# A transformer layer on one core: from all experts for every token to two experts per token, in seats of 128 rows

## What is computed

```python
x = x + _layernorm(attention(_layernorm(x), wq, wk, wv, wo, biases))
x = x + _layernorm(ffn(_layernorm(x)))

def ffn(x):                                # H = 256, I = 176, E = 8, K = 2
    probs = softmax(einsum('bsh,he->bse', x, Wr))
    topk_w, topk_idx = top_k(probs, K)
    topk_w = topk_w / sum(topk_w)
    combine = einsum('bsk,bske->bse', topk_w, one_hot(topk_idx, E))
    g = einsum('bsh,ehi->besi', x, Wg)     # the reference: all experts, all tokens
    u = einsum('bsh,ehi->besi', x, Wu)
    y = einsum('besi,eih->besh', silu(g) * u, Wd)
    return einsum('bse,besh->bsh', combine, y)
```

## Time and profile before

| | |
|---|---|
| median of three runs | 2106.59 us |
| the profiled execution | 2106.23 us, its span 2104.5 us |
| TensorE busy | 2035.6 us, 97% of the span |
| VectorE, GpSimd, ScalarE busy | 84%, 73%, 67% |
| mean granted clock of TensorE | 0.986 |
| last `add_out` of attention | starts 1854.25 us after the span's start |
| first of the 44 expert steps | starts at 1885.56 us |

### The profile page before, as it was taken

The page is one execution under the profiler, slowest core; times in us unless marked ns, Lnnn a source line. Parts: engine busy times, 40 slices in busy tenths (PEclk is TensorE's granted clock), DMA queues, the critical chain, the costliest instruction groups (busy, mean ns, idle before and its releaser), DMA issues.

```text
span 2104.5 us, 32745 instructions
## 1 busy us (share of the span) xinstructions
PE 2035.6 (97%) x11188; PEld 1755.3 (83%) x11188; DVE 1775.5 (84%) x2651; ACT 1404.8 (67%) x2575; POOL 1546.5 (73%) x1329
## 2 busy tenths in 40 slices
PE   7999999999999999999999999999999999849998
PEld 5888888888888888888888888888888888738887
DVE  6889889988989888988999898989898889865553
ACT  5777767776777667776776677776777677624443
POOL 2679778886879777877787787877797678846333
PEclk9999999999999999999999999999999999969999
DMA  4667657766667666765777666766676567730000
GB/s 101 159 154 177 160 141 164 171 164 161 147 155 177 154 146 159 180 159 140 165 169 160 148 160 151 176 154 148 153 181 157 136 151 171 165 112 1 11 11 21
DMA packets 216584, 298.24 MB, mean 142 GB/s; under 512 B 44897, under 2 KB 85345, under 8 KB 216417
## 3 DMA queue, kind: packets, MB, share of 16 engines
q1 hardware_dynamic: 216416, 296.15, 59.9%
HBM read 25.46 MB, written 2.10 MB: 13 GB/s over the span
## 4 chain that ended last, share of the span: by engine, by line
PE 74%; SPq 8%; DVE 7%; POOL 5%; ACT 3%; DMA 2%; issue 1%; POOLq 0%; DVEq 0%; ACTq 0%
PE ps_a L617 16%; PE ps_s L498 13%; PE ps_s L500 13%; PE ps_s L499 13%; PE ps_a L618 8%; SPq L317 7%; POOL pT_both L410 4%; PE ps_a L498 2%; PE ps_a L500 2%; PE ps_a L499 2%; DVE probs L1086 2%; ACT probs L821 2%; DVE part_max L1067 1%; PE ps_a L751 1%; PE ps_a L754 1%
## 5 line engine op out<-in xcount | busy, mean ns | idle before, releaser
L410 POOL TENSOR_TENSOR pT_both<-pT,pT_both 128x512 fp32r<-128x512 f32 x1024 | 1301.1, 1301 | 350.4 <-ACT pT_both L834 348.2
L617 PE MATMUL ps_a<-pT_both,v_hi 128*128 128x512 f32 x2048 | 741.5, 395 | 3.8 <-POOL pT_both L410 3.6
L834 ACT ACTIVATE pT_both<-pT 128x512 fp32r<-128x512 f32 x1024 | 610.7, 630 | 195.5 <-DMA pT<-probs 163.2
L821 ACT ACTIVATE probs<-ps_s,shift 128x1024 f32<-128x1024 f32 x512 | 566.3, 1109 | 259.0 <-DVE shift L1076 258.5
L1086 DVE STREAM_TRANSPOSE probs<-probs 128x1024 f32<-128x1024 f32 x512 | 619.1, 1229 | 55.0 <-ACT probs L821 54.2
L1067 DVE TENSOR_REDUCE part_max<-ps_s 128x1 f32<-128x1024 f32 x512 | 612.4, 1215 | 16.1 <-PE ps_s L500 9.5
L618 PE MATMUL ps_a<-pT_both,v_lo 128*128 128x256 f32 x2048 | 574.5, 281 | 0.0
L617 PEld LDWEIGHTS ps_a<-pT_both,v_hi 128*128 128x128 f32 x2048 | 385.3, 188 | 86.8 <-POOL pT_both L410 3.7
L498 PE MATMUL ps_s<-kT_hi,qT_hi 128*128 128x512 f32 x1024 | 405.0, 396 | 11.6 <-ACT probs L821 8.2
L500 PE MATMUL ps_s<-kT_hi,qT_lo 128*128 128x512 f32 x1024 | 403.6, 394 | 0.0
L499 PE MATMUL ps_s<-kT_lo,qT_hi 128*128 128x512 f32 x1024 | 403.0, 394 | 0.0
(11 more groups left out here) (159 smaller groups left out, 2859.5 us busy)
## 6 DMA issues: line engine op xcount, KB each, us to landing
pT<-probs SPq DMA_DIRECT2D x2048, 128.0 KB, 2.5
pT<-in_L_attn_x SPq DMA_DIRECT2D x4, 512.0 KB, 5.7
codes<-in_L_attn_wk_codes SPq DMA_DIRECT2D x16, 128.0 KB, 2.4
scales<-in_L_attn_wk_scales SPq DMA_DIRECT2D x64, 32.0 KB, 3.0
codes<-in_L_attn_wo_codes SPq DMA_DIRECT2D x16, 128.0 KB, 2.3
scales<-in_L_attn_wo_scales SPq DMA_DIRECT2D x64, 32.0 KB, 1.9
x<-in_L_attn_x SPq DMA_DIRECT2D x4, 512.0 KB, 7.1
layer_out<-x SPq DMA_DIRECT2D x8, 256.0 KB, 2.1
```

The lines of the kernel that those rows point to most:

```text
L410: pool.tensor_tensor(pT_lo[:, p, :].rearrange("p (i n) -> p i n", i=Q4), pT[:, s % 2, g, :, t:t + 2, :].rearrange("p i t q -> p i (t q)"), ...
L617: nc.tensor.matmul(out_both, v_hi[:, k, h % 2, :], both[:, :, :, t, :], start=k == 0, stop=False)
L821: nc.scalar.activation(out, src, ACT.Exp, bias=shift[:, s % SLOTS, r:r + 1], scale=SCALE, accum_out=sums[:, s % SLOTS, r, g:g + 1])\
L834: nc.scalar.activation(pT_hi[:, p, :].rearrange("p (i n) -> p i n", i=Q4), pT[:, s % 2, g, :, t:t + 2, :].rearrange("p i t q -> p i (t q)" ...
```

## The change

The tokens are put into two parts of eight tiles of 128 rows. For each part the router works out, for each token, its two experts and a row for each in a table in device memory. The table of a part has 23 seats of 128 rows (2·8 + 8 − 1: enough however the tokens fall), each of which belongs to one expert; both parts have 46. GpSimd sends each token's normed row to its two rows with indirect DMAs (`send`: two for each tile, 32 in all). Then a loop over the 46 seats loads a seat, turns it (`turn_x`), reads the seat's expert into a register (`expert_of`), multiplies with that expert's weights at an address from the register (`gate_up`: six matmuls of 352 columns), turns the hidden rows (`turn_h`), multiplies down (`down`: six of 256 columns) and stores the seat. GpSimd fetches each token's two result rows (`fetch`, 32 indirect DMAs), ScalarE and VectorE weigh and sum them, and the last norm follows. All 46 seats are computed, also those that no token has.

Around it: the tables are cleared with 46 DMAs in the first 23 attention steps. The expert weights are split during heads 3, 5, 7, 9, 11 and 13, in 32 units with one high part on ScalarE and one low part on GpSimd each, and put in device memory by seven DMAs; GpSimd loads them back at the end of attention. The residual x1 is loaded six steps before attention's end. The norm and router of the first part follow attention's drain; those of the second part stand before the seat loop up to the logits, and in its first ten turns for the rest.

```diff
+    PART_TILES = [(0, 8), (8, 8)]
+    BATCHES = [(0, 8), (8, 4), (12, 4)]
+    SEATS = [2 * n + E - 1 for _, n in PART_TILES]
+    FIRST_SEAT = [sum(SEATS[:u]) for u in range(PARTS)]
+    NS = sum(SEATS)
+    XR = 4
+    YR = 8
+    GR = 4
+    YS = 4
...
+        SESSIONS = [(3, 0, 5), (5, 5, 10), (7, 10, 15), (9, 15, 21), (11, 21, 27), (13, 27, 32)]
...
+  def load_unit(j):
+      kind, c, e = UNITS[j]
+      if j == 0:
+          sp.wait_ge(x_cleared, 16 * NS)
+      wait(sp, "piece_lo", j - 1)
+      if kind == "gu":
+          for n, w in enumerate((wg, wu)):
+              sp.dma_start(unit_raw(j)[:, n * I:(n + 1) * I], w[e, c * P:(c + 1) * P, :])\
+                  .then_inc(raw_loaded[j % 2], 16)
+      else:
+          sp.dma_start(unit_raw(j), wd[e, c * KD:(c + 1) * KD, :]).then_inc(raw_loaded[j % 2], 16)
...
+      if s == 0 and h - 1 in [head for head, _, _ in SESSIONS]:
+          store_units([head for head, _, _ in SESSIONS].index(h - 1))
+      if unit_at(n, 0) is not None:
+          load_unit(unit_at(n, 0))
+      if n == HALVES - NH + 2:
+          wait(sp, "pv_done", PAIRS_KT * (HALVES - NH))
+          for g in range(NCH):
+              rows = slice(g * TPC, (g + 1) * TPC)
+              sp.dma_start(x1[:, rows, :], xv[:, rows, :]).then_inc(res_loaded[g], 16)
       turn_blocks(n)
+      for seat in range(2 * n, min(2 * n + 2, NS)):
+          if seat == 0:
+              sp.wait_ge(sm["zeros_set"], 1)
+          u, k = part_of(seat), seat - FIRST_SEAT[part_of(seat)]
+          sp.dma_start(x_rows[u][k * P:(k + 1) * P, :], zeros).then_inc(x_cleared, 16)
...
+  def load_seat(j):
+      u = part_of(j)
+      if j == FIRST_SEAT[u]:
+          sp.wait_ge(x_sent[u], 32 * PART_TILES[u][1])
+      wait(sp, "xg_t", j - XR + 1)
+      n = j - FIRST_SEAT[u]
+      sp.dma_start(xg[:, j % XR, :], x_rows[u][n * P:(n + 1) * P, :]).then_inc(xg_loaded[j % XR], 16)
+  def store_seat(j):
+      u = part_of(j)
+      n = j - FIRST_SEAT[u]
+      sp.wait_ge(sm["y_copied"], j + 1)
+      sp.dma_start(y_rows[u][n * P:(n + 1) * P, :], y_sb[:, j % YS, :]).then_inc(y_stored[j % YS], 16)
...
+  for n in range(NS + 9):
+      if n < NS:
+          load_seat(n)
+      if n >= 9:
+          store_seat(n - 9)
...
+  def unit_lo(j):
+      rows = slice(0, unit_shape(j)[0])
+      pool.wait_ge(sm["piece_hi"], j + 1)
+      pool.tensor_tensor(stage[rows, 1, unit_cols(j)], unit_raw(j), full(stage[rows, 0, unit_cols(j)]),
+                         ALU.subtract).then_inc(sm["piece_lo"], 1)
...
+  def send(u):
+      if u == 0:
+          pool.wait_ge(x_cleared, 16 * NS)
+      pool.wait_ge(sm["row_done"], u + 1)
+      for t in tiles_of(u):
+          pool.wait_ge(sm["xn2_done"], t + 1)
+          for k in range(2):
+              pool.indirect_dma_start(x_rows[u][:, :], bass.IndirectOffsetOnAxis(row[:, t, k:k + 1], 0),
+                                      acc[:, t, :], None).then_inc(x_sent[u], 16)
+  def fetch(t):
+      u = part_of_tile(t)
+      if t == PART_TILES[u][0]:
+          for b in range(YS):
+              pool.wait_ge(y_stored[b], 16 * len(range(b, FIRST_SEAT[u] + SEATS[u], YS)))
+      wait(pool, "ysum_done", t - GR + 1)
+      for k in range(2):
+          pool.indirect_dma_start(yg[:, t % GR, k, :], None, y_rows[u][:, :],
+                                  bass.IndirectOffsetOnAxis(row[:, t, k:k + 1], 0))\
+              .then_inc(yg_loaded[t % GR], 16)
+  send(0)
+  send(1)
+  for t in range(TT):
+      fetch(t)
...
+  def turn_x(j):
+      if not 0 <= j < NS:
+          return
+      pe.wait_ge(xg_loaded[j % XR], 16 * (j // XR + 1))
+      wait(pe, "xs_lo_done", j)
+      for c in range(DC):
+          last = nc.tensor.transpose(ps_x[:, c * P:(c + 1) * P], xg[:, j % XR, c * P:(c + 1) * P],
+                                     ident[:, :])
+      last.then_inc(sm["xg_t"], 1)
+  def expert_of(j):
+      if not 0 <= j < NS:
+          return
+      u = part_of(j)
+      n = j - FIRST_SEAT[u]
+      if n == 0:
+          pe.wait_ge(sm["expert_ready"], u + 1)
+      expert_at[j] = pe.value_load(expert_i[0:1, u, n:n + 1], min_val=0, max_val=E - 1)
+  def gate_up(j):
+      if not 0 <= j < NS:
+          return
+      if j == 0:
+          pe.wait_ge(gu_loaded, 64)
+          wait(pe, "acc_done", HALVES)
+      wait(pe, "xs_lo_done", j + 1)
+      wait(pe, "h_done", j - 1)
+      for c in range(DC):
+          hi, lo = xs_hi[:, j % 2, c * P:(c + 1) * P], xs_lo[:, j % 2, c * P:(c + 1) * P]
+          w_h, w_l = (w[:, c, bass.ds(expert_at[j], 1), :].rearrange("p a n -> p (a n)")
+                      for w in (gu_hi, gu_lo))
+          last = product3(ps_gate(j), hi, lo, w_h, w_l, first=c == 0, last=c == DC - 1)
+      last.then_inc(sm["gate_ready"], 1)
...
+  def down(j):
...
+      pe.wait_ge(sm["hs_lo_done"], j + 1)
+      wait(pe, "y_copied", j)
+      for k in range(2):
+          hi, lo = hs_hi[0:KD, j % 3, k * P:(k + 1) * P], hs_lo[0:KD, j % 3, k * P:(k + 1) * P]
+          w_h, w_l = (w[0:KD, k, bass.ds(expert_at[j], 1), :].rearrange("p a n -> p (a n)")
+                      for w in (d_hi, d_lo))
+          last = product3(ps_y, hi, lo, w_h, w_l, first=k == 0, last=k == 1)
+      last.then_inc(sm["down_done"], 1)
...
+  turn_rows(0)
+  turn_rows(1)
+  route(0)
+  route(1)
+  count_all(0)
+  count_places(0)
+  turn_rows(2)
+  turn_rows(3)
+  route(2)
+  route(3)
+  expert_of(0)
+  turn_x(0)
+  for n in range(NS + 3):
+      turn_h(n - 2)
+      turn_x(n + 1)
+      gate_up(n)
+      expert_of(n + 1)
+      if n == 4:
+          count_all(1)
+      if n == 7:
+          count_places(1)
+      down(n - 3)
...
+  seat_hi(0)
+  for n in range(NS + 4):
+      hidden_hi(n - 2)
+      seat_hi(n + 1)
+      seat_out(n - 4)
+      gate(n)
+      if n in POST:
+          weigh(POST[n])
+      if n == OUT + 1:
+          out_std(0)
+      if OUT + 2 <= n < OUT + 6:
+          for t in range(2):
+              out_norm(2 * (n - OUT - 2) + t)
+  for t in range(8, 12):
+      weigh(t)
...
+      if n == HALVES - 1:
+          finish_chunk(0)
+      if n == HALVES:
+          finish_chunk(1)
+          first_eps(0)
+      if n == HALVES + 1:
+          first_scale(0)
+          add_norm(0)
+  add_norm(1)
...
+  row_scale(0)
+  finish_chunk(2)
+  rows_lo(0)
+  rows_lo(1)
+  sum_logits(0)
+  sum_logits(1)
+  shift_logits(0)
+  beaten(0)
+  tie_broken(0)
+  choose(0)
+  seat_starts(0)
+  seat_rows()
+  take_places(0)
+  rows_of(0)
+  seat_experts(0)
+  finish_chunk(3)
+  first_eps(1)
+  first_scale(1)
+  add_norm(2)
+  add_norm(3)
+  row_scale(1)
+  rows_lo(2)
+  rows_lo(3)
+  sum_logits(2)
+  sum_logits(3)
+  shift_logits(1)
+  seat_lo(0)
+  for n in range(NS + 4):
+      hidden_lo(n - 2)
+      seat_lo(n + 1)
+      hidden(n)
+      if n == 0:
+          beaten(1)
+      if n == 1:
+          tie_broken(1)
+      if n == 2:
+          choose(1)
+      if n == 4:
+          seat_starts(1)
...
+      if n == 8:
+          rows_of(1)
...
+      if n in POST:
+          combine(POST[n])
...
-  pre_all(dve, pre)
...
-  for n in range(STEPS + LAG):
-      if n < STEPS:
-          hidden(n)
-      hooks(n, pre, post)
```

899 lines of the change are left out of this document (521 added, 378 removed).

## The result

Four runs of the changed kernel gave 2158.8 to 2160.5 us, median 2159.6; before beside them had 2107.4. The ratio is 1.0247 (1.023 to 1.0265): slower by 52 us, where I forecast 2084 and a range up to 2132. Two later sets of runs of the same file gave 2134.1 and 2134.3, ratios 1.0132 (1.0111 to 1.0152) and 1.0135 (1.0109 to 1.0161).

What follows compares the result with a forecast made beforehand. TensorE bounds attention, and its matmul columns the expert stage. Loop start 1915 + 3 low clock + 127 seats + 32 end + 4 attention = 2081 us span, forecast as 2084 (1.1% less); 8-in-10 range 2054 to 2132.

Steps and rivals of the forecast that it cites:

- I take 4 us; below 0, above 25: Attention: SyncE's 105 added issues and the weight-splitting work mostly fit in free time, costing 4 us.
- Rival 3: Attention: SyncE falls behind with its added issues, 25 us instead of 4, giving 2105, the same; chance 0.06.
- From the anchor to the loop: Last `add_out` to the seat loop: norm, routing and sends, with VectorE finishing last; loop starts at about 1915.
- The adds: Before the loop: VectorE's adds beside GpSimd's indirect DMAs are not slowed; none taken, 10 us left in the range.
- The seats: Seat loop: 2.6 us a seat as the mean, 49 turns until the last `down`, 127 us, plus 3 at low clock.
- the ring: Seat loop: `down` waits until ScalarE empties the one bank `ps_y`, behind the next seat's transposes' evacuation; 2.3 us a seat.
- Rival 1: Seat loop: TensorE's register instructions set the pace, 3.5 us a seat, 2128, slower; chance 0.27.
- Rival 2: Sends and gathers: GpSimd's indirect DMAs take 2.5 us; loop starts 15 us later, last 16 add 21; 2120; chance 0.10.
- The end: After the last `down`: store, 16 gathers of the second part, combine, norm and final store take 32 us.

Runs made afterwards that it cites:

- second trace: Trace of the changed kernel run again with nothing edited: median 2134.1 us, seat loop 110.2 us without stalls.
- units_late: Against the changed kernel, unit conversions moved to the step's end, unit loads and session stores behind the turning DMAs; 2132.4 us, ratio 1.0124.

## Why the prediction was wrong

1. **Attention, "I take 4 us; below 0, above 25"**: the step that failed. It measured 65.8 us in the first trace and 63.2 in the second. I counted SyncE's issues and found that one high and one low part a step "fit in the free quarters of ScalarE and GpSimd". They do: 0.5 and 1 us. I priced the two instructions and not their waits. `unit_hi`'s wait for `pv_done` stood in the changed kernel, though not among the lines of it that I showed; the trace of before says when the previous head's values end; and everything of ScalarE's half is queued behind it. It cost 5.1 us each, six times, shown by moving it. The bias row, 7.8 us three times, could not be read from before, where it never took over 1.43. It came with the sessions and went with them, and moving it to ScalarE took it away as well. I had no term for the clock either, which fell behind both waits.
2. **Rival 3, SyncE falls behind, 25 us**: at most some 9 us of the 63, in head 15, where four large loads stand together and spreading them gave 5 to 6.5 us, and in head 1, where it is not shown to be SyncE. Heads 0 and 2 are at before's length (103.7 for 103.5, 118.3 both) although SyncE issues two clears a step through head 0 and most of head 2, as in head 1.
3. **From the anchor to the loop, 60 us**: 60.7, but not behind VectorE as I had it: the sends took longer (point 6), and the first seat's transposes waited 1.05 us for their load. The adds were right: I took nothing for indirect DMAs beside VectorE's adds. The four adds of the bias took 1.42 us, as they do alone, with a send starting among them, and the two rounds of residuals 1.67 and 1.64 beside sends, 1.66 without:

```profile
1951.07 1.42 DVE L1417 TENSOR_TENSOR acc<-acc,vb_sum 128x256 f32<-128x256 f32 x4
1951.16 1.28 POOL L604 DMA_INDIRECT x_rows<-acc,row  x1 [32.04 <-DVE row L1613]
...
1979.63 0.69 PE L871 MATMUL ps_s<-ident,xg 128*128 128x128 f32 x2 [1.05 <-DMA xg<-x_rows]
```

4. **The seats**: the ring was forecast at 2.3 us and measured 2.40. I added 0.3 for VectorE's routing in the first turns and combining in the last, and that was too much: only two intervals of 3.0 to 3.2 us at each end of the loop stand out. So 120 us for 130.
5. **Rival 1, registers, 3.5 us a seat** (0.27): false. Leaving out the read and the computed addresses gives 2.40 − 2.27 = 0.13 us a seat, 5 us in all. Whether the read plays a part in the stalls (theory R) stays open.
6. **Rival 2, indirect DMAs at 2.5 us** (0.10): false. One takes 0.97 us and the next starts 0.30 later; I had 1.2 for each. The sends also pause for 2.0 us or more after every seven, so sixteen are 24 us for my 19, nearly hidden behind VectorE and TensorE. The last sixteen gathers have no such pause: 20 us.
7. **The end**, 32: 33.
8. **Not foreseen**: the stalls in the loop, 24 us in the first trace. Without them the time is 2134, still slower and still above my range, by attention alone: 2081 + 59 (attention) − 10 (seats) + 2 (the rest) = 2132, the second trace's span.

The chance of "slower" was 0.30, spread over rivals of the new part. The two costs that make it slower even without the stalls lay in the part that the change only visits.

## What to carry to other kernels

Work put "in the free quarter" of an in-order engine costs only its own duration if its operands and its output buffer are free when its turn comes: read from the trace when the last reader of a borrowed buffer ends, and put the work behind an instruction that waits for the same event anyway (5.1 us at the front of the step; at its end that half was back at before's 12.6, and what the six heads still paid for the work, some 8 us together, lay elsewhere). When an edit's time fits the forecast, look at the stage that it names before you believe it, and run the unedited kernel beside it: `units_late` hit its number with attention unchanged.
